# A decoder layer on one core: the first attention's output projection joined with the second attention's queries, and the experts' weights loaded while the last list entries are scattered

## The reference

```python
x = x + _L0_attn_ref(_layernorm(x), q_heads, k_heads, v_heads, output_proj)
x = x + _L0_xattn_ref(_layernorm(x), ctx_1024, W_q, W_k, W_v, W_o, b_o)
x = x + _L0_ffn_ref(_layernorm(x), gate_W, gate_b, W1, b1, g1, be1, W2, b2, g2, be2)
# _L0_attn_ref:  softmax(mask(q k^T / sqrt(32))) v, then @ output_proj.T ; q = x @ q_heads.T, and so on
# _L0_xattn_ref: Q = x @ W_q, K = ctx @ W_k, V = ctx @ W_v, softmax without mask, @ W_o + b_o
# _L0_ffn_ref:
gate_scores = xf @ gate_W + gate_b
topk_scores, topk_idx = jax.lax.top_k(gate_scores, 2)
weights = jax.nn.softmax(topk_scores, axis=-1)
h = relu(layernorm(xf @ W1[e] + b1[e]) * g1[e] + be1[e])
y = layernorm(h @ W2[e] + b2[e]) * g2[e] + be2[e]
out = sum over the token's two experts of weight * y, + xf
```

## Time and profile before

| what | value |
|---|---|
| median of 3 runs | 4449.33 us (4442.33 to 4449.73) |
| the profiled execution's own time | 4446.99 us |
| its span | 4445.3 us |
| mean granted TensorE clock | 0.94 |
| busy: PE, PEld, DVE, ACT, POOL | 4010.5, 2473.0, 2727.0, 2095.5, 2589.9 us |
| stages by the timeline | "out1" from 1072, "q2" from 1186, "kv2" from 1334, `finish` from 3595, `experts` from 3897 to the end |

### The profile page before, as it was taken

How to read it: one execution, slowest core, us unless ns; L and a number is a source line. 1 busy time by engine, 2 the same in 40 slices (tenths; PEclk the granted TensorE clock), 3 DMA queues, 4 the chain that set the end, 5 groups by cost and what they waited for, 6 DMA issues and landing times. The chain is left out here.

```text
span 4445.3 us, 60825 instructions
## 1 busy us (share of the span) xinstructions
PE 4010.5 (90%) x21522; PEld 2473.0 (56%) x21522; DVE 2727.0 (61%) x4963; ACT 2095.5 (47%) x3870; POOL 2589.9 (58%) x963
## 2 busy tenths in 40 slices
PE   6997999997788998999999999999999967349997
PEld 5874555554676886444444444444444445238885
DVE  4435777772453334877777777777777525336765
ACT  2112555553122111566666666666666634226665
POOL 0003455454000001699999999999999935618887
PEclk8996999998898998899999999999999978669998
DMA  4546454422555556122222222222222036434444
GB/s 145 179 156 145 107 113 90 107 48 87 206 193 180 174 171 170 34 58 58 58 58 58 58 58 58 58 58 58 58 58 58 6 144 137 76 105 81 80 83 62
DMA packets 275062, 432.66 MB, mean 97 GB/s; under 512 B 31689, under 2 KB 132041, under 8 KB 268618
## 3 DMA queue, kind: packets, MB, share of 16 engines
q1 hardware_dynamic: 251050, 390.23, 33.6%
q0 software_dynamic: 19776, 36.85, 4.9%
q10 hardware_dynamic: 3968, 2.10, 0.2%
HBM read 258.57 MB, written 170.52 MB: 97 GB/s over the span
## 5 line engine op out<-in xcount | busy, mean ns | idle before, releaser
L881 DVE TENSOR_REDUCE cross_neg_max<-cross_scores 128x1 f32<-128x512 f32 x2048 | 1264.8, 676 | 396.0 <-PE cross_scores L708 395.9
L665 POOL TENSOR_TENSOR cross_partial<-cross_partial,cross_probs 128x2048 f32<-128x2048 f32 x320 | 1465.6, 4580 | 66.7 <-ACT cross_probs L832 29.6
L832 ACT ACTIVATE cross_probs<-cross_shifted 128x512 f32<-128x512 f32 x2048 | 1074.1, 606 | 742.3 <-PE cross_shifted L720 707.6
L708 PE MATMUL cross_scores<-cross_k_stack,cross_q_stack 96*128 96x512 f32 x2048 | 875.9, 437 | 39.7 <-DVE cross_neg_max L881 27.4
L720 PE MATMUL cross_shifted<-cross_q_stack,cross_k_stack 98*128 98x512 f32 x2048 | 850.7, 420 | 13.9 <-ACT cross_probs L832 6.1
L720 PEld LDWEIGHTS cross_shifted<-cross_q_stack,cross_k_stack 98*128 98x128 f32 x2048 | 387.1, 190 | 385.5 <-issue 233.6
L708 PEld LDWEIGHTS cross_scores<-cross_k_stack,cross_q_stack 96*128 96x128 f32 x2048 | 395.2, 193 | 286.6 <-DVE cross_neg_max L881 224.1
L832 ACT ACTIVATE self_probs<-self_shifted 128x512 f32<-128x512 f32 (+3 forms) x768 | 358.8, 492 | 348.4 <-PE self_shifted L723 266.9
L881 DVE TENSOR_REDUCE self_neg_max<-self_scores 128x1 f32<-128x512 f32 (+3 forms) x768 | 388.0, 547 | 187.1 <-PE self_scores L708 96.2
L736 PE MATMUL cross_out<-cross_probs,cross_v 128*32 128x512 f32 x4096 | 492.7, 598 | 0.0
L708 PE MATMUL self_scores<-self_k_stack,self_q_stack 96*128 96x512 f32 (+3 forms) x768 | 308.3, 423 | 21.0 <-DMA self_k_stack<-k_hi 9.8
(11 more groups left out here) (268 smaller groups left out, 6113.9 us busy)
## 6 DMA issues: line engine op xcount, KB each, us to landing
cross_k_stack<-k_hi SPq DMA_DIRECT2D x30, 1024.0 KB, 20.0
kv_x_in<-in_ctx SPq DMA_DIRECT2D x16, 1024.0 KB, 5.5
k_hi<-kv_out_hi SPq DMA_DIRECT2D x64, 256.0 KB, 2.6
k_lo<-kv_out_lo SPq DMA_DIRECT2D x64, 256.0 KB, 3.2
v<-kv_out_n SPq DMA_DIRECT2D x64, 256.0 KB, 2.3
cross_v<-v SPq DMA_DIRECT2D x32, 512.0 KB, 25.1
self_q_stack<-q_hi SPq DMA_DIRECT2D x30, 512.0 KB, 6.9
self_k_stack<-k_hi SPq DMA_DIRECT2D x30, 512.0 KB, 15.2
```

Source lines behind the costliest of these rows:

```text
L665: nc.gpsimd.tensor_tensor(total, total, own, ALU.add).then_inc(pool_added.sem, 1)
L708: mm = nc.tensor.matmul(scores[at][:, 0:width], q_st[0:96, w, h, q0:q0 + P], k_st[0:96, w, h, half * WIDE:half * WIDE + width], start=True ...
L832: nc.scalar.activation(probs[:, e % NE % PB, h, f:], shifted[n % SHIFTED][:, f:], ACT.Exp).then_inc(exped.sem, 1)
L881: nc.vector.tensor_reduce(neg_max[:, q % 2, column(a), half:half + 1], scores[n % (SLOTS * ROUNDS) % AHEAD][:, 0:width], AX.X, ALU.max, ne ...
```

## The change

- "out1" and "q2" become one phase, `bridge`. It is built like `finish`: the output projection runs two chunks ahead, one chunk's result stays in SBUF for the normalisation and the queries, and is also stored to `x1`. The output weight is turned into four separate PSUM tiles and split by quarters. The normalisation moves from DVE to ACT. `W_k` and `W_v` are loaded and split inside this phase (chunks 2 and 4).
- "kv2" has no `load_weights`; SP begins with its first two chunks.
- `finish` scatters the entries of chunks 0 to 5. The entries of chunks 6 and 7 (`LATE = 2`, 32 indirect DMAs) go to POOL's stream in `experts`, ahead of `gather(0)`.
- SP in `experts` begins with the rows and `W2`, reads four beginnings into registers, waits for the 32 scatters, and then issues all 35 lists.
- ACT and DVE split `W2` ahead of the first step. POOL's wait for the rows of `g2` and `be2` moves to their first use in `gain(0)`. DVE's `gates_of(1)` moves from s = -2 to s = 2.

```diff
-def project_out(nc, name, attn_t, weight, bias, residual, out, ident):
+def bridge(nc, name, attn_t, out_w, residual, x1, q_w, q_out, q_scale, next_w, next_hi, next_lo, ident, neg_half):
+        @block.sync
+            def load(c):
+                if c >= 3:
+                    sp.wait_ge(x_stored[c % 3], 16 * (c // 3))
+                    sp.wait_ge(normed, TPC * (c - 2))
+                sp.dma_start(x_in[:, c % 3], tiles_of(residual)[c]).then_inc(loaded[c % 3], 16)
...
+            for c in range(CHUNKS):
+                sp.wait_ge(added, TPC * (c + 1))
+                sp.dma_start(tiles_of(x1)[c], x_in[:, c % 3]).then_inc(x_stored[c % 3], 16)
+                if c + 3 < CHUNKS:
+                    load_attention(c + 3)
+                    load(c + 3)
+                for n in range(HG):
+                    sp.wait_ge(out_lo_ready, HG * c + n + 1)
...
+        @block.scalar
+            for k in range(KT):
+                act.wait_ge(w_turned, k + 1)
+                nc.scalar.activation(ow_hi[:, k], q_acc[k][:, :], ACT.Copy).then_inc(ow_hi_ready, 1)
+            attention_high(0)
...
+            for c in range(CHUNKS):
+                after(act, q_ready, HG * c)
+                for t in range(TPC):
+                    act.wait_ge(turned_ready, TPC * c + t + 1)
+                    nc.scalar.activation(xt_hi[:, :, t * P:(t + 1) * P], turned[t % 2][:, :, :], ACT.Copy).then_inc(hi_ready, 1)
+                if c + 1 < CHUNKS:
+                    normalise(c + 1)
+                if c + 3 < CHUNKS:
+                    attention_high(c + 3)
+                if c in (2, 4):
+                    next_high(c // 2 - 1)
+                for n in range(HG):
+                    act.wait_ge(q_ready, HG * c + n + 1)
+                    after(act, q_stored[n], 32 * c)
+                    nc.scalar.activation(out_hi[:, n], q_acc[n][:, :], ACT.Copy, scale=q_scale).then_inc(out_hi_ready, 1)
...
+        @block.vector
+            for c in range(CHUNKS):
+                for t in range(TPC):
+                    dve.wait_ge(hi_ready, TPC * c + t + 1)
+                    nc.vector.tensor_tensor(xt_lo[:, :, t * P:(t + 1) * P], turned[t % 2][:, :, :],
+                                            xt_hi[:, :, t * P:(t + 1) * P].bitcast(F32), ALU.subtract).then_inc(lo_ready, 1)
+                    if t == 0 and c + 1 < CHUNKS:
+                        variance(c + 1)
+                    if t and c + 2 < CHUNKS:
+                        add_projection(c + 2, t - 1)
+                if c + 1 < CHUNKS:
+                    scales(c + 1)
+                if c + 2 < CHUNKS:
+                    add_projection(c + 2, TPC - 1)
+                if c + 3 < CHUNKS:
+                    attention_low(c + 3)
+                if c in (2, 4):
+                    next_low(c // 2 - 1)
+                for n in range(HG):
+                    dve.wait_ge(out_hi_ready, HG * c + n + 1)
+                    after(dve, q_stored[n], 32 * c)
+                    nc.vector.scalar_tensor_tensor(out_lo[:, n], q_acc[n][:, :], q_scale, out_hi[:, n].bitcast(F32),
+                                                   ALU.mult, ALU.subtract).then_inc(out_lo_ready, 1)
...
+        @block.tensor
+            for t in range(2 * TPC):
+                project_tile(t // TPC, t % TPC)
+            for c in range(CHUNKS):
+                for t in range(TPC):
+                    turn_tile(c, t)
+                    if t and c + 2 < CHUNKS:
+                        project_tile(c + 2, t - 1)
+                if c + 2 < CHUNKS:
+                    project_tile(c + 2, TPC - 1)
+                pe.wait_ge(lo_ready, TPC * (c + 1))
+                if c == 0:
+                    pe.wait_ge(qw_lo_ready, 1)
+                for n in range(HG):
+                    queries(c, n)
@@ project ("kv2"), SP
+            if split:
+                first_loads(sp)
@@ finish, POOL
-                if c:
+                if 0 < c <= CHUNKS - LATE:
                     scatter(c - 1)
-            scatter(CHUNKS - 1)
-            pool.wait_ge(listed, 16 * TILES * EXPERTS)
+            pool.wait_ge(listed, 16 * (TILES - LATE * TPC) * EXPERTS)
@@ experts, SP
+            load_rows(0)
+            for e in range(3):
+                load_second(e)
+            load_rows(1)
...
+            load_rows(3)
+            begin = lambda s: sp.value_load(table[0:1, s, 1:2], min_val=0, max_val=EXPERTS * BATCH * SEQ - TOK)
+            first = [begin(s) for s in range(FIRST_LISTS)]
+            sp.wait_ge(listed, 16 * LATE * TPC * EXPERTS)
             for s in range(STEPS):
-                at = sp.value_load(table[0:1, s, 1:2], min_val=0, max_val=EXPERTS * BATCH * SEQ - TOK)
+                at = first[s] if s < FIRST_LISTS else begin(s)
@@ experts, POOL
+            for t in range(LATE * TPC):
+                for e in range(EXPERTS):
+                    pool.indirect_dma_start(lists, bass.IndirectOffsetOnAxis(place[:, t, e:e + 1], 0),
+                                            pairs[:, t, e, :], None).then_inc(listed, 16)
             gather(0)
-            pool.wait_ge(rows_in[2], 16 * EXPERTS)
-            pool.wait_ge(rows_in[3], 16 * EXPERTS)
@@ experts, DVE
                 if s == -2:
                     gates_of(0, slice(0, FIRST_LISTS))
+                if s == 2:
                     gates_of(1, slice(FIRST_LISTS, STEPS))
```

More of the change, by code:

```diff
@@ L28 @@
 STEP_ROWS = 256
+LATE = 2
 STEPS = 2 * BATCH * SEQ // STEP_ROWS + EXPERTS - 1
@@ L1054, in finish, with project_tile @@
-def finish(nc, name, attn_t, out_w, out_b, residual, gate_w, gate_b, w1, xn, out, lists, w_hi, w_lo, table, valid, ident, neg_half):
+            def project_tile(c, t):
+                if t == 0:
+                    pe.wait_ge(a_lo_ready, c + 1)
+                after(pe, added, TPC * c + t - 1)
+                i = 0
+                for part, w in ((a_hi, ow_hi), (a_hi, ow_lo), (a_lo, ow_hi)):
+                    for k in range(KT):
+                        mm = nc.tensor.matmul(acc[t % 2][:, :], part[:, k, t * P:(t + 1) * P], w[:, k, :], start=i == 0, stop=i == 11)
+                        i += 1
+                mm.then_inc(acc_ready, 1)
@@ new lines, in turn_tile, with queries @@
+            def turn_tile(c, t):
+                pe.wait_ge(normed, TPC * c + t + 1)
+                after(pe, lo_ready, TPC * c + t - 1)
+                for k in range(KT):
+                    mm = nc.tensor.transpose(turned[t % 2][:, k, :], x_n[:, c % 2, t, k * P:(k + 1) * P], ident[:, :])
+                mm.then_inc(turned_ready, 1)
+            def queries(c, n):
+                after(pe, out_lo_ready, HG * (c - 1) + n + 1)
+                i = 0
+                for w, part in ((qw_hi, xt_hi), (qw_hi, xt_lo), (qw_lo, xt_hi)):
+                    for k in range(KT):
+                        mm = nc.tensor.matmul(q_acc[n][:, :], w[:, k, n * P:(n + 1) * P], part[:, k, :], start=i == 0, stop=i == 11)
+                        i += 1
+                mm.then_inc(q_ready, 1)
@@ L1062, in finish @@
+def finish(nc, name, attn_t, out_w, out_b, residual, gate_w, gate_b, w1, xn, out, lists, w_hi, w_lo, table, valid, pairs, place, ident, neg_half):
     CHUNKS = BATCH * SEQ // CH
@@ L1506, in _, with experts @@
             nc.tensor.matmul(count_ps[:, :], all_ones[:, :], counted[:, TILES, :], start=True, stop=True).then_inc(counts_ready, 1)
-def experts(nc, w2, vectors, xn, lists, w1_hi, w1_lo, table, valid, out, ident):
+def experts(nc, w2, vectors, xn, lists, w1_hi, w1_lo, table, valid, pairs, place, out, ident):
     TT = STEP_ROWS // P
```

338 lines of the change are left out of this document (202 added, 136 removed).

## The result

| | before | after |
|---|---|---|
| median | 4445.93 us (4 runs) | 4389.47 us (4 runs) |
| the profiled execution's own time | 4446.99 us | 4395.31 us |
| its span | 4445.3 us | 4393.6 us |

The ratio is 0.9871, with a 95% interval from 0.9852 to 0.9891: 56 us less, where the forecast had 50. In time, 4399 us were forecast, with a range from 4381 to 4421, and 4389.47 were measured. (A fourth run of the kernel before has moved its median from 4449.33 to 4445.93 us.) The profiled execution of after is the slowest of its four and shows 51.7 us of it. One execution of `changed` (21105 us) and one of `both` (5552 us), two runs of the experiments, were slow ones and do not enter their ratios.

A forecast was written before the change was run, and what follows sets the result against it. PE alone bounds steady stretches such as "kv2"; elsewhere it waits, chiefly at seams. 30.3 us (`bridge` and "kv2") plus 20.0 (seam to `experts`) cut the span from 4445.3 to 4395.0; with 4.0 for the median, 4399 us, range 4381 to 4421.

The forecast's parts named there:

- Bridge, the beginning: Start of `bridge`: first product 4.1 us earlier, PE waits of 4.4 us before chunks 1 and 2, restarts costing 2.4 us.
- Bridge, the period: Steady loops of `bridge`: 24.0 us each for loops 1 to 5, then 39.2 us for loops 6 and 7.
- The term of 22.5: Joined phase up to the start of "kv2": "kv2" begins at 1311.8 instead of 1334.3, 22.5 us gained.
- Barrier: End of `finish`: from DVE's last instruction to the first scatter in `experts`, 1.2 us taken from 0.3 to 3 us.
- Scatters: Start of `experts`: 32 scatters at 1.265 us, 40.5 us, plus 7.2 us for four blocked by DVE's `W2` splits.
- Landing: In `experts`, from the end of the scatters to the start of the lists: 4.2 us.
- From the lists on: In `experts`, lists' start at 3911.3 to the marker, from which PE runs steadily (3969.1 before), at 3949.1.
- Seam term 20.0: From `finish` into `experts`: the marker, from which PE runs steadily, comes 20.0 us earlier, despite lists starting 13.2 us later.
- the prediction's own sign of being wrong: At the start of `experts`: the first list over 55 us after the end of `finish` would show the forecast wrong.
- The bridge keeps the handshake: Rival, 8%: in `bridge`, six loops each pay 4.4 + 2.4 us waiting for the attention's split, 41 us; time 4440.
- The seam gives nothing: Rival, 10%: in `experts`, loads and scatters slow each other or the 6.1 us gap returns; lists 20 us later, 4419.
- Every scatter takes 2.87: Rival, 3%: all 32 scatters in `experts` take 2.87 + 0.3 us, 54 us more; the kernel is slower, 4453 us.

The follow-up runs named there:

- changed: The changed kernel measured once more, beside the last experiments: 4382.12 us, ratio to before 0.9869.
- both: The changed kernel with the edits of `a2` and `quiet` together: 4374.97 us, ratio to before 0.9853.
- a2: Against the changed kernel, `bridge` splits attention chunk 1 into a second, free pair of buffers, and chunks 1 and 2 earlier: 4374.83 us, ratio to before 0.9853.
- kv_keep: The changed kernel, but "kv2" loads and splits its weights in its own block again, as before: 4390.15 us, ratio to before 0.9899.
- late3: The changed kernel, but chunks 5, 6 and 7 are scattered in `experts` (48 scatters instead of 32): 4393.08 us, ratio to before 0.9897.
- quiet: The changed kernel, but three of DVE's four `W2` splits wait for the scatters' landing, and row and column loads come later: 4378.59 us, ratio to before 0.9863.
- gates_early: The changed kernel, but `gates_of(1)` is back at s = -2, so DVE takes all 35 lists' weights before the first scale: 4390.95 us, ratio to before 0.9894.
- seam_only: The kernel before with only the late scatters and the new order at the beginning of `experts`: 4418.39 us, ratio to before 0.9947.
- cols_last: The changed kernel, but SP issues the two 4-byte-element column loads behind all other weights in `experts`: 4382.72 us, ratio to before 0.9872.
- a2_cols: The changed kernel with the edits of `a2` and `cols_last` together: 4373.13 us, ratio to before 0.9847.
- late1: The changed kernel, but only chunk 7's entries are scattered in `experts` (16 scatters instead of 32): 4387.81 us, ratio to before 0.9883.
- bridge_only: The kernel before with only the joined phase and "kv2" without weights, `finish` and `experts` as before: 4407.72 us, ratio to before 0.9922.

## Why the prediction was right, step by step

- **Bridge, the beginning.** First product 14.1 us after the first DMA forecast, 13.8 measured; waits of 4.4 and 4.4 forecast, 4.39 and 3.52 measured. `a2` shows that they lay on the path: without them the phase is 7.0 us shorter. The restart was taken too dear: 2.4 us for chunk 0, where 1.3 was measured (12.6 us against 11.3 at the steady pace).
- **Bridge, the period.** 24.0 forecast, 23.95 to 23.96 measured in each of loops 1 to 5; the last two loops 39.2 forecast, 39.0 measured. The seam behind them 5.1 forecast, 5.2 measured (from the end of PE's last product, 1305.8, to 1310.99). The term of 22.5 came out as 25.9 because chunk 0 took 12.6 us instead of 13.7, the second wait was 0.9 shorter and loop 0 ended 24.9 us after its chunk 2's first product, instead of 25.5. Other executions of the same phase had 236.6 to 239.3 us, so 23.4 to 26.0 gained.
- **"kv2".** 7.8 forecast; 7.8 in the profiled pair. Its length has two values in these runs, 398.4 to 398.8 and 400.7 to 400.8 us, so 8 to 10 gained. `kv_keep` returned it: 408.1.
- **Barrier: the step that failed.** "The barrier costs something between 0.3 us and the 3 us" and 1.2 taken: it was 6.0, outside these bounds, since POOL's drain of 7.901 us ended last. Where the drain is hidden (`late3`), the 1.2 is right to 0.1. The forecast had kept the 6.08 us gap out of its value as something without a releaser; by the reading above it was the same cost.
- **Scatters.** A pitch of 1.265 us forecast, 1.263 measured. Four blocked ones forecast, three measured, at 1.7 us each (2.66 to 2.73 against 0.96): the fourth split fell behind the last scatter. 47.7 forecast for the chain, 45.3 measured; 42.0 with one blocked (`quiet`).
- **Landing: mis-sized.** 4.2 us from the last scatter's end to the lists forecast, 9.0 measured. The 4.2 was the remainder of a seam with the wrong barrier in it. It follows the loads still under way, by the landing times in the traces: in the change the last scatter lands 8.9 us after its end, and so does SP's last load. Over the eleven profiles with `LATE` at 2 or 3, the time from the last scatter's end to the lists was 7.7 to 10.3 us where SP's last load before them landed 6.9 to 11.0 us after that end (the change, `changed`, `kv_keep`, `a2`, `gates_early`), 4.8 to 5.8 where it landed 4.5 to 5.2 after (`seam_only`, `both`, `cols_last`, `a2_cols`), 2.9 where it landed 1.4 after (`quiet`), and 3.0 where all loads had landed 7.0 us before (`late3`). (In `late1` SP was late, and the lists say nothing of the landing.)
- **From the lists on.** 37.8 us to the marker forecast, 35.9 measured, and 33.2 in the second profile. DVE's wait for the 31 lists is gone; `gates_early` brings it back, with a wait of 12.26 us and a marker 7.2 us later.
- **The sum.** Seam term 20.0: 14.1 in the first profiled pair, 22.1 by `seam_only` and 21.8 by its trace. In that pair the first scatter began 6.6 us after DVE's end instead of 1.2, and the landing took 4.8 us more: together 10.2 us too good a forecast. The chain of scatters (2.4) and the way from the lists to the marker (1.9) gave 4.3 back: 5.9, the difference of 20.0 and 14.1. The rest is in the baseline: in the kernel before the stretch from DVE's last instruction to the marker was 110.9 us with a `finish` of 262.9, and 117.6 in `bridge_only` with one of 248.9. So the prediction's own sign of being wrong came true for the seam (lists at 60.9 us instead of 53.1, with 55 as the limit; 58.4 in `changed`), and that the term of 20.0 still came out near 22 is luck: an old way to the marker that is longer than in the one profile of before makes up for a new one that is longer than forecast. The total was 50 where 56 to 57 were measured, 6 us of 4390, by errors of both signs; that the first profiled pair comes to 51.7 against 50.3 is luck in part, for 4.4 us of it lie in `finish`, which the change was not to touch.
- **Rivals.** "The bridge keeps the handshake" is excluded: no PE wait for `a_lo` in loops 1 to 5. "Every scatter takes 2.87" is excluded: 29 of 32 took 0.96. "The seam gives nothing" is excluded by `seam_only`, though both of its conditions were met in part: loads and scatters did slow each other, and by the reading above the 6.1 us gap came back as a drain; lists started 7.8 us later than worked out, not 20.

The Trainium skill, SBUF — State Buffer, "Who interferes with whom", infers that descriptor generation is untouched by a DVE instruction with two SBUF inputs. The trace differs: a scatter waits for the end of such an instruction, and `quiet`, which moves three of the four instructions away, keeps one long scatter. The Trainium skill, DMA: Bandwidth & Descriptors, "Anatomy of one DMA", gives about 2.0 us for the fixed cost; the 2.9 us of `quiet` are near it, and the 9.0 us with 2 MB of loads under way are not.

## What to carry to other kernels

Where PE alone bounds a phase, one steady loop of a phase with the same matmuls forecasts its period: here 24.0 us, and 23.95 came. The uncertainty sits in the seams. There, look at what each queue does between its last instruction and the barrier: DVE waiting "for PEq" was really waiting for POOL's drain. And when a wait is removed by moving loads beside it, ask what the moved loads land beside next: here 2 MB of rows delayed either the last scatter or the first gather, and moving them from one to the other gained nothing that could be measured.

## What the runs showed of the hardware that was not expected

- POOL's drain at the end of `finish` grew by 0.082 us with each scatter: 6.594, 7.901 and 9.207 us after 80, 96 and 112. With 128 there was one stall behind the 113th, of 6.08 us in the kernel before and 5.99 in `bridge_only`, and a drain of 1.286 us. At the end of `experts` the drain was 3.733 us whether the phase had issued 140, 156, 172 or 188 indirect DMAs.
- From the end of the last 128-row, 8-byte scatter to the lists it took 2.9 to 3.0 us with no row loads under way and 4.8 to 10.3 us with loads under way, about as long as these loads took to land.
- The second of two 8 KB loads with 4-byte elements held SP's queue for 14.3 to 20.7 us beside the scatters and behind the first weight loads (ten profiles), for 8.9 us in the kernel before, behind the same weight loads but with no scatters beside it, and for 7.8 and 6.7 us in `cols_last` and `a2_cols`, where scatters did run beside it but it came behind all other loads. So the scatters alone are not the cause; what it is stays open.
- `finish` took 262.9, 258.5 and 257.5 us in three profiled executions and 248.1 to 250.6 in the others, whatever the kernel. In the change's first profile and in `a2` the difference is one late load: DVE waits 10.5 and 8.5 us for `finish_x_in`, and PE 6.0 and 5.2 us for DVE's addition, which no other profile has to that length. In the kernel before most of it lies elsewhere, in waits of 7.3 to 7.8 us on ACT, DVE and PE near 3838 for which the profile shows no releaser.
